# Four runs of 30 neighbouring partitions instead of interleaved ones for the rows of a combination matmul

## The reference

```python
w = jnp.einsum('rb,bio->rio', att, basis)      # att (2, 30), basis (30, 512, 512)
```

## Time and profile before

| | |
|---|---|
| median of 3 runs | 5510.89 us (5507.32 to 5512.34) |
| the profiled execution | 5506.21 us |
| its span | 5504.4 us |
| PE / DVE / ACT / POOL busy | 77% / 54% / 39% / 26% of the span |
| DMA | 924.32 MB, mean 168 GB/s |
| `order_basis` loads | 128 x 480 KB, issued 21.8 to 403.2 us |
| matmuls that read them | 512, from 44.8 to 445.6 us |

### The profile page before, as it was taken

How to read it: one execution, slowest core, us unless ns; L and a number is a source line. 1 busy time by engine, 2 the same in 40 slices (tenths; PEclk the granted TensorE clock), 3 DMA queues, 4 the chain that set the end, 5 groups by cost and what they waited for, 6 DMA issues and landing times. The chain is left out here.

```text
span 5504.4 us, 70253 instructions
## 1 busy us (share of the span) xinstructions
PE 4216.8 (77%) x22571; PEld 3378.6 (61%) x22571; DVE 2992.2 (54%) x6700; ACT 2139.4 (39%) x3450; POOL 1455.9 (26%) x1380
## 2 busy tenths in 40 slices
PE   5766989799897710663389897989889897989533
PEld 2334868688786610542179773988579774988311
DVE  3435754377685564434755445554455435554588
ACT  0111213222337800220133564347533664347566
POOL 1322112211340007774433004310233004310243
PEclk9887999899998855665589995999789995999755
DMA  8994237722896603666955226532555127532354
GB/s 235 295 273 152 77 114 250 238 72 71 330 401 244 235 20 90 121 127 157 330 177 162 76 94 231 162 112 91 194 171 162 72 96 234 162 106 92 136 195 161
DMA packets 493679, 924.32 MB, mean 168 GB/s; under 512 B 107759, under 2 KB 108039, under 8 KB 492632
## 3 DMA queue, kind: packets, MB, share of 16 engines
q1 hardware_dynamic: 296076, 532.11, 29.2%
q0 software_dynamic: 118272, 237.34, 15.8%
q10 hardware_dynamic: 79088, 151.77, 7.6%
HBM read 597.24 MB, written 322.46 MB: 167 GB/s over the span
## 5 line engine op out<-in xcount | busy, mean ns | idle before, releaser
L684 PE MATMUL hidden_O<-hidden_xh,w_hi 128*128 128x256 f32 (+1 forms) x2560 | 728.8, 285 | 0.3 <-DVE hidden_xl L1057 0.2
L685 PE MATMUL hidden_O<-hidden_xh,w_lo 128*128 128x256 f32 (+1 forms) x2560 | 717.0, 280 | 0.0
L686 PE MATMUL hidden_O<-hidden_xl,w_hi 128*128 128x256 f32 (+1 forms) x2560 | 716.8, 280 | 0.0
L684 PE MATMUL output_O<-w_hi,output_hh 128*128 128x512 f32 (+1 forms) x1264 | 503.3, 398 | 56.5 <-DVE output_hl L1950 56.5
L1829 POOL DMA_INDIRECT hidden_agg<-edge_sums,edge_where x316 | 339.6, 1075 | 756.8 <-DVE hidden_xin L1876 605.6
L1860 ACT ACTIVATE hT<-hidden_O,hidden_b 128x256 f32<-128x256 f32 (+1 forms) x640 | 247.6, 469 | 659.1 <-PE hidden_O L686 659.1
L685 PE MATMUL output_O<-w_hi,output_hl 128*128 128x512 f32 (+1 forms) x1264 | 502.4, 397 | 0.0
L686 PE MATMUL output_O<-w_lo,output_hh 128*128 128x512 f32 (+1 forms) x1264 | 502.1, 397 | 0.0
L684 PEld LDWEIGHTS hidden_O<-hidden_xh,w_hi 128*128 128x128 f32 x2560 | 484.4, 189 | 1.5 <-DVE hidden_xl L1057 1.4
L685 PEld LDWEIGHTS hidden_O<-hidden_xh,w_lo 128*128 128x128 f32 x2560 | 485.2, 190 | 0.0
L686 PEld LDWEIGHTS hidden_O<-hidden_xl,w_hi 128*128 128x128 f32 x2560 | 483.3, 189 | 0.0
(11 more groups left out here) (376 smaller groups left out, 10014.4 us busy)
## 6 DMA issues: line engine op xcount, KB each, us to landing
hidden_xin<-g SPq DMA_DIRECT2D x156, 512.0 KB, 4.0
g<-output_y SPq DMA_DIRECT2D x156, 512.0 KB, 2.7
order_basis<-in_L_gnn_basis SPq DMA_DIRECT2D x128, 480.0 KB, 16.5
edge_sums<-message_res SPq DMA_DIRECT2D x160, 256.0 KB
edge_sums<-relation_res SPq DMA_DIRECT2D x80, 256.0 KB, 2.0
order_x<-in_x SPq DMA_DIRECT2D x39, 512.0 KB, 17.9
normed<-order_y ACTq DMA_DIRECT2D x39, 512.0 KB, 9.2
root_xin<-normed SPq DMA_DIRECT2D x39, 512.0 KB, 3.7
```

Source lines behind the costliest of these rows:

```text
L684: eng.matmul(out, a_hi, b_hi, start=start, stop=False)
L685: eng.matmul(out, a_lo, b_hi, start=False, stop=False)
L686: return eng.matmul(out, a_hi, b_lo, start=False, stop=stop)
```

## The change

Two slices of partitions are written differently, that of the coefficients and that of the basis rows. (b, quarter) lay in partition 4b + quarter and lies in partition 30 * quarter + b.

```diff
@@ -339,7 +339,7 @@
                     for r in range(RELATIONS):
                         for quarter in range(4):
                             at = SIDE - 4 + r * SIDE + quarter
-                            eng.dma_start(spread[n][quarter:BASIS_ROWS:4, at:at + 1], att[r].rearrange("(b one) -> b one", one=1),
+                            eng.dma_start(spread[n][quarter * BASES:(quarter + 1) * BASES, at:at + 1], att[r].rearrange("(b one) -> b one", one=1),
                                           allow_slow_non_contiguous=True).then_inc(s[f"att{n}"], 16)
...
                     for quarter in range(4):
-                        eng.dma_start(ba_t[i % W][quarter:BASIS_ROWS:4, :, :], src_[:, quarter, half * HALF:(half + 1) * HALF, :]).then_inc(ba[i % W], 16)
+                        eng.dma_start(ba_t[i % W][quarter * BASES:(quarter + 1) * BASES, :, :], src_[:, quarter, half * HALF:(half + 1) * HALF, :]).then_inc(ba[i % W], 16)
```

## The result

Five runs gave a median of 5552.44 us (5543.35 to 5567.55) beside 5508.29 us for the kernel before in as many runs (5500.00 to 5512.34): a ratio of 1.0084, 95% interval 1.0064 to 1.0103. The changed kernel is slower, by 44 us. The forecast was 5533, the range 5485 to 5585.

The account below looks back on a forecast made before the run. The prediction took the DMA engines to bound the front. The profiled 5506.2 us plus 22 us exposed (27/32 of 26) gave 5528.2, forecast as a median of 5533 us; range 5485 to 5585.

Parts of the forecast that it names:

- The front is bound by the DMA engines, only the front changes, everything behind shifts as a block.: Order phase, until about 446 us: DMA share 0.99 to 1.01 from 36 to 350 us; later phases only shift.
- The destination sets the rate; neighbours are slower; the source costs nothing.: Basis loads: writing 30 neighbouring partitions instead of interleaved ones lowers 218 GB/s to 200, 26 us more.
- Rival (a): Basis loads: where rows are read sets the 218 GB/s, so nothing changes, 5511 us; chance 0.28.
- Rival (b): Basis loads, 36 to 350 us: interleaving is the bad pattern, neighbours reach 252 GB/s, 33 us less, 5478; chance 0.17 with anything faster.
- Rival (c): Basis loads: 30 neighbours fall to the bad end, 159 GB/s, 90 us more, 5601 us; chance 0.10.
- 252 GB/s for 64 neighbours, as a bound for 30.: Basis loads: the `w_hi`/`w_lo` rate as the good end, 249.6 us, 39 us less than now.
- 200 GB/s, half of the x rate.: Basis loads: a narrow run reaches half of what serves 128 partitions; 314.6 us, 26 us more.
- 62.9 MB at the rates of 36 to 70 us.: All basis loads in the front: 288.6 us at 218 GB/s, 314.6 us at 200 GB/s.
- 27/32 of it exposed.: Front: 27 of 32 half blocks count on the path, so 22 of the 26 us are exposed.
- Coefficient loads at 0, covered by the row loads.: Start of the front: 16 issues done by 20.3 us, while row loads need the engines until 35.9; cost 0.
- The clock at 0.: Long stage: PE's granted clock may fall, but its 62 us of slack cover it; 13 us without that cover.

Follow-up runs that it names:

- e1: Kernel before, but each basis load reads its 240 rows from one stretch of 480 KB, destination still interleaved: 5514.3 us beside 5513.2.
- e2: Changed kernel, but each basis load reads its 240 rows from one stretch of 480 KB, destination 30 neighbouring partitions: 5549.8 us beside 5513.2.
- e3: Kernel before with each basis load cut into two of 15 matrices, in steps of 8 partitions, coefficients alike: 5524.4 us beside 5513.2.
- e4: Kernel before with each basis load cut into two of 15 matrices, each into 15 neighbouring partitions, coefficients alike: 5663.9 us beside 5513.2.
- e6: Kernel before, interleaved, with basis loads of 4 rows per matrix instead of 8 (256 loads of 240 KB): 5487.4 us against 5514.6, ratio 0.9943.
- e7: Kernel before with quarters 0 and 1 in the lower 60 partitions in steps of 2, 2 and 3 in the upper: 5545.2 us beside 5514.6.
- e12: Changed kernel with basis loads of 4 rows per matrix and quarters in the order 0, 2, 1, 3: ratio 1.0013 to the kernel before.
- e9: Changed kernel with each basis load cut into two of 4 rows per matrix: 5541.4 us, ratio 1.0041 to the kernel before.
- e5: Kernel before with only the 16 coefficient loads going into runs of 30 neighbours, basis still interleaved: 5500.0 us beside 5514.6.
- e8: Kernel before with three quarters in steps of 3 over partitions 0 to 89, the fourth side by side in 90 to 119: 5543.0 us beside 5514.6.
- e10: e6 with the two broadcasts of edge rows moved ahead of the coefficient loads on SP's queue: 5477.0 us against 5517.7, ratio 0.9915.

## Why the prediction was right, and where not

The sign and the bound were right, the size was half: +22 us forecast, +44 measured. 5552 lies inside the stated range, which was wide enough for both signs, and 5 us outside the forecast's own range of 5524 to 5547.

- *The front is bound by the DMA engines, only the front changes, everything behind shifts as a block.* Right: share 0.99 to 1.01 as before, +50.0 us in the front, +49.9 in the span.
- *The destination sets the rate; neighbours are slower; the source costs nothing.* Right for these loads, shown by e1 to e4. Rival (a) is out as the cause of the 218. Rival (b) had the sign wrong, but e6 shows that 252 GB/s could be had, in the interleaved layout. Its idea of engines that work in step and meet is not shown; e6, e7 and e12 (254, 198 and 216 GB/s) agree with it. Rival (c) priced 30 neighbours at 159 GB/s; they move at 192, and it takes runs of 15 to fall to 118.
- *252 GB/s for 64 neighbours, as a bound for 30.* Misread. The loads of `w_hi` and `w_lo` go in turn into partitions 0 to 63 and 64 to 127 (`half` is the innermost loop at L743), so at 128 KB each and 252 GB/s they go from one to the other every 0.5 us. The earlier trace rows therefore show a queue that changes its place that often, not what one run of 64 gives, and the factor of 0.63 built on them has no basis.
- *200 GB/s, half of the x rate.* The size was off: 192, which at 62.9 MB is 39 us and not 26. It was a guess between 159 and 252, and the reason given (the nearest value) had no mechanism behind it. No run shows that a narrow run reaches half of what serves all 128 partitions; what the runs show is 192 GB/s for 30 neighbours and 118 for 15. It also took x at its peaks of about 400; in the changed kernel the x slices of the stretch from 403 us show 364 to 381, and half of that is 182 to 190. The level within a run is about 184 to 187 GB/s by the narrow slices.
- *62.9 MB at the rates of 36 to 70 us.* Too small as well. SP's queue took 46 us more of engine time, 7 more than the 39 that the measured rates of 36 to 70 us give. In the mixed stretch the interleaved loads run faster than alone, and the runs gain less: the 13 basis slices of the earlier trace rows average 231 GB/s, the 19 after it 194, both with some bytes of stores. (That stores and x keep the engines out of step there is argued, not shown.) The rows for this were in the earlier trace rows; I used alone.
- *27/32 of it exposed.* Wrong in direction: the time from first to last matmul grew by 55.1 us (455.9 against 400.8), which is all of the 46 us and more, so nothing was hidden at the end. ACT's stores took 2 us more of the engines; the remaining 7 us were not traced. PE's waits for basis rows grew from 79.1 to 94.0 us.
- *Coefficient loads at 0, covered by the row loads.* Wrong. These 16 issues stand ahead of the row loads on SP's queue, so nothing covers them: their 6.2 us are a gain, of which 1.2 go to the slower first four loads (9.0 to 10.2 us). I read "done by 20.3 us" and did not ask what waited for it.
- *The clock at 0.* It fell a little, 0.85 to 0.83 in the long stage and 0.81 to 0.76 from 403 us, with PE waiting more; PE's busy time in the whole span grew by 4.7 us (4216.8 to 4221.5). Not separated further.

## What to carry to other kernels

When several loads of few partitions stand in a queue, look at which partitions successive loads write and how often that changes, not at what the whole set of loads covers; here the rate in narrow slices of the DMA view showed it as a level with bumps (184 GB/s, with 225 to 238 every 5 us). Smaller loads that change their place more often can be faster than large ones (217 to 254 GB/s here, 193 to 205 in runs), and so can the same loads in another order (205 to 216 from e9 to e12), where SP's issue time (0.84 us each in steps of partitions) stays below the time they move (0.97 us for 240 KB at 254 GB/s). And what stands first in an issue queue can be on the path even if it moves only 120 bytes: here the 16 coefficient loads, issued in 7.03 instead of 13.3 us, brought the first matmul 6.4 us forward (e5).

## What was not expected of the hardware

SP takes about twice as long to issue a load whose partitions go in steps: 774 ns against 403 for a coefficient load (30 x 4 bytes), and at least 835 ns against 323 for a basis load. With steps of 2 it is 835 ns as well (e7), and the full 256 loads of e6 had a median of 836. In e8, where every fourth load goes into 30 neighbours, no basis load was issued in under 590 ns, so it is not the load's own pattern alone.

Three loads of four in steps of 3 gave no more than all four in steps of 4: e8 showed 219 GB/s from 38 to 70 us, the kernel before 218 from 36 to 70, and e8 fell to 172 to 182 once for each side-by-side load. Whether one slow destination holds all DMA engines back was not shown.

What stays open: runs of 15 gave 118 GB/s, but runs of 30 a level of about 184 to 187 and not twice as much. Why the runs lose more than e7 does beside x and the stores. And why e10 shows 270 GB/s from 36 to 54 us, where e6 with the same loads shows 254 from 36 to 60, was not tried.
